# A second pair of PSUM banks for the attention output, and the weight sums moved from head pair 2 to head pair 7

## The reference, cut to what matters

```python
qkv = grouped_linear(x, w_qkv, None)              # 8 groups, 128 -> 384
attn = softmax((q * D**-0.5) @ k^T)               # 16 heads, D = 64
x = layernorm(x + grouped_linear(attn @ v, w_proj, b_proj))
def _weight_quant(w):
    scale = 1.0 / clip(mean(abs(w)), 1e-05)
    return clip(round(w * scale), -1.0, 1.0) / scale
def _bitlinear(x, w): return einsum('bsi,oi->bso', _act_quant(x), _weight_quant(w))
x = layernorm(x + _bitlinear(silu(_bitlinear(x, w_gate)) * _bitlinear(x, w_up), w_down))
```

## Time and profile before

| | us |
|---|---|
| median of 2 runs | 2174.44 |
| the profiled execution, device time | 2174.42 |
| its span on the slowest core (core 2), first to last instruction | 2171.6 |
| PE busy / ACT busy / DVE busy | 1345.0 / 969.3 / 924.0 |
| attention and its projections, from about 190 to 1183 us of the span | about 990 |
| FFN, from about 1196 us on | about 975 |

### The profile page before, as it was taken

One profiled execution on the slowest core, in us unless ns is written; L12 is line 12 of the kernel. 1 busy time (PEld: TensorE's weight loads), 2 busy tenths in 40 slices (PEclk: granted clock), 3 DMA queues, 4 the chain that ended last, 5 costly groups with the idle time before them and its releaser, 6 DMA issues.

```text
span 2171.6 us, 20607 instructions; the slowest of 8 cores (2159.1 to 2171.6 us)
## 1 busy us (share of the span) xinstructions
PE 1345.0 (62%) x5502; PEld 462.6 (21%) x5502; DVE 924.0 (43%) x1742; ACT 969.3 (45%) x1079; POOL 44.6 (2%) x84
## 2 busy tenths in 40 slices
PE   0057666466656665045663599964999847676682
PEld 0011111111111111011111244421444312222231
DVE  1138840463548344385515644444444441203023
ACT  2167778477866877037782122255121352011011
POOL 0000000000000000001000000000000000000000
PEclk9999888688877888568886799987999978898896
DMA  6789950124752587745721533334244425676672
GB/s 190 215 237 311 321 178 1 34 79 128 200 143 78 168 225 218 212 122 169 216 61 37 143 78 78 76 99 136 51 95 97 107 97 155 162 208 182 183 210 82
DMA packets 371458, 314.02 MB, mean 145 GB/s; under 512 B 296593, under 2 KB 298641, under 8 KB 369298
## 3 DMA queue, kind: packets, MB, share of 16 engines
q1 hardware_dynamic: 339712, 234.97, 41.8%
q10 hardware_dynamic: 23186, 48.38, 6.3%
q0 software_dynamic: 8448, 29.37, 3.5%
HBM read 161.49 MB, written 83.89 MB: 113 GB/s over the span
## 4 chain that ended last, share of the span: by engine, by line
PE 36%; ACT 21%; DMA 13%; DVE 12%; SPq 8%; issue 7%; ACTq 2%; DVEq 1%; POOL 0%; POOLq 0%
PE ps L84 36%; ACT A L84 21%; DVE A L84 8%; SPq L84 7%; DMA A<-wg 3%; DMA wdt_sb<-wdqT_s 2%; DVE ln_sb L84 2%; ACTq L84 2%; DMA wtstage<-wdq_s 2%; DMA A<-wproj 1%; DMA xre_f<-xp_s 1%; DVE h L84 1%; DMA wdqT_s<-wtstage 1%; DMA A<-wu 1%; DMA A<-x 1%
## 5 line engine op out<-in xcount | busy, mean ns | idle before, releaser
L84 ACT ACTIVATE A<-ps,cst_sb 128x1024 bf16<-128x1024 f32 (+1 forms) x544 | 573.7, 1087 | 276.4 <-DVE A L84 143.6
L84 PE MATMUL ps<-A,A 128*65 128x512 bf16 (+1 forms) x2048 | 527.8, 427 | 271.9 <-ACT A L84 258.5
L84 PE MATMUL ps<-wg_sl,xqT 128*128 128x512 bf16 x1024 | 266.4, 407 | 114.4 <-DVE h L84 101.1
L84 PE MATMUL ps<-wdt_sb,hqT 128*128 128x512 bf16 x1024 | 242.4, 396 | 106.6 <-DMA wdt_sb<-wdqT_s 50.2
L84 PEld LDWEIGHTS ps<-A,A 128*65 128x65 bf16 (+1 forms) x2048 | 124.8, 105 | 673.1 <-issue 673.1
L84 ACT ACTIVATE A<-ps,scg 128x512 f32<-128x512 f32 x128 | 87.9, 687 | 332.2 <-PE ps L84 310.2
L84 DVE SCALAR_TENSOR_TENSOR h<-ps,scu,A 128x512 bf16<-128x512 f32 x128 | 96.1, 750 | 217.3 <-ACT A L84 213.1
L84 DVE TENSOR_SCALAR A<-A,wsc 128x1024 f32<-128x1024 f32 x96 | 72.2, 753 | 212.4 <-DMA A<-wg 100.9
L84 DVE TENSOR_SCALAR A<-A 128x1024 f32<-128x1024 f32 (+1 forms) x208 | 144.3, 694 | 32.1 <-DVE A L84 18.0
L84 PEld LDWEIGHTS ps<-wg_sl,xqT 128*128 128x128 bf16 x1024 | 103.9, 103 | 252.8 <-issue 146.3
L84 PEld LDWEIGHTS ps<-wdt_sb,hqT 128*128 128x128 bf16 x1024 | 100.8, 101 | 248.2 <-issue 145.8
(11 more groups left out here) (66 smaller groups left out, 702.2 us busy)
## 6 DMA issues: line engine op xcount, KB each, us to landing
A<-wg SPq DMA_DIRECT2D x64, 512.0 KB, 6.5
A<-wu SPq DMA_DIRECT2D x64, 512.0 KB, 5.7
A<-wd SPq DMA_DIRECT2D x64, 512.0 KB, 6.7
wdt_sb<-wdqT_s SPq DMA_DIRECT2D x128, 256.0 KB, 3.2
hq_s<-h ACTq DMA_DIRECT2D x16, 1024.0 KB, 3.9
A<-x SPq DMA_DIRECT2D x16, 512.0 KB, 7.7
xt_s<-A POOLq DMA_DIRECT2D x16, 512.0 KB, 4.2
A<-xt_s ACTq DMA_DIRECT2D x16, 512.0 KB, 3.3
```

The lines of the kernel that those rows point to most:

```text
L84: ins = getattr(eng, meth)(*args, **kw)
```

## The change

Three things are edited. The PV matmuls and the four copies use PSUM banks 4 and 5 for even head pairs and banks 6 and 7 for odd ones, and the first PV matmul of a pair waits only until the copies of the pair before the last are done (`c_pve` less 1). The weight sums (`emit_wsum`) are taken after pair 7 of query chunk 1 and no longer after pair 2; since `drain_wq` runs only once they are taken, and only for p < 7, the units begin at pair 0 of query chunk 2. And since the sums use PSUM bank 6, waits are added: the sums wait for all copies, the first PV matmul and the projection for `wsc`.

```diff
     def emit_wsum():
         wait("tensor", "c_bpb", 1)
+        wait("tensor", "c_pve", c("c_pve"))
         wait("tensor", "c_wma", c("c_wma"))
...
         for p in range(8):
+            pvb = 2048 if p % 2 == 0 else 3072
...
                 if kc == 0:
-                    wait("tensor", "c_pve", c("c_pve"))
-                if kc == 0 and p == 0:
+                    wait("tensor", "c_pve", max(0, c("c_pve") - 1))
+                    wait("tensor", "c_wsc", c("c_wsc"))
+                if kc == 0 and p <= 1:
                     wait("tensor", "c_radd", c("c_radd"))
                 va = A4[:, kc * 1040:(kc + 1) * 1040]
-                em("tensor", "matmul", ps[0:65, 2048:2560],
+                em("tensor", "matmul", ps[0:65, pvb:pvb + 512],
...
-            em("scalar", "copy", arp[0:64, :], ps[0:64, 2048:2560])
-            em("scalar", "copy", arp[64:128, :], ps[0:64, 2560:3072])
+            em("scalar", "copy", arp[0:64, :], ps[0:64, pvb:pvb + 512])
+            em("scalar", "copy", arp[64:128, :], ps[0:64, pvb + 512:pvb + 1024])
...
-            if qc == wsum_qc and p == 2:
+            if qc == wsum_qc and p == 7:
                 emit_wsum_once()
...
             xre = A0[:, par * 1024:(par + 1) * 1024]
             wait("tensor", "c_rcp", c("c_rcp"))
+            wait("tensor", "c_wsc", c("c_wsc"))
```

More of the change, by code:

```diff
@@ L682, in build @@
                    start=(kc == 0), stop=(kc == T - 1))
-                em("tensor", "matmul", ps[0:65, 2560:3072],
+                em("tensor", "matmul", ps[0:65, pvb + 512:pvb + 1024],
                    va[:, 65 * (2 * p + 1): 65 * (2 * p + 1) + 65],
@@ L700, in build @@
             arp = A8[:, p * 512:(p + 1) * 512]
-            em("scalar", "copy", arp[0:64, :], ps[0:64, 2048:2560])
-            em("scalar", "copy", arp[64:128, :], ps[0:64, 2560:3072])
+            em("scalar", "copy", arp[0:64, :], ps[0:64, pvb:pvb + 512])
+            em("scalar", "copy", arp[64:128, :], ps[0:64, pvb + 512:pvb + 1024])
             em("scalar", "copy",
                A9[row:row + 1, 0:512].rearrange("r (q tc) -> r tc q", tc=4),
-               ps[64:65, 2048:2560])
+               ps[64:65, pvb:pvb + 512])
             em("scalar", "copy",
                A9[row:row + 1, 512:1024].rearrange("r (q tc) -> r tc q", tc=4),
-               ps[64:65, 2560:3072], inc=("c_pve", 1))
+               ps[64:65, pvb + 512:pvb + 1024], inc=("c_pve", 1))
             if attn_lvl < 2:
```

## The result

| | before | after |
|---|---|---|
| median, us | 2175.22 (8 runs) | 2260.37 (9 runs) |
| ratio, 95% interval | 1 | 1.0389 [1.0369, 1.0409] |
| span of the slowest core in the profiled execution | 2171.6 (core 2) | 2265.3 (core 0) |

The change makes the kernel 3.9 per cent slower. 2270 us were forecast, in a range of 2250 to 2290.

A forecast was written before the change was run, and what follows sets the result against it. ACT paces the attention, but chunk 2's end waits for weight quantization units and transposes. Sums -2.0, chunk 2 -30.3, chunk 3 +58.8 and tail +69.0 give +95.5 on 2174.4: 2270 us, range 2250 to 2290.

The forecast's parts named there:

- The banks: 0: Pair changes in attention: new banks gain 0, since ACT's copies stand ahead of the exp that the first PV matmul needs.
- The bound of -39 us: Lower bound for the banks: some 1.4 us of ACT idle time taken away at each of 28 pair changes.
- The bound of +3 us: Upper bound for the banks: one more semaphore to look at per pair, at most a tenth of a us.
- The weight sums: -2.0: Chunk 1: 2.4 us go at pair 2, 0.4 come back at pair 7, so it ends 2.0 us earlier.
- Chunk 2: reciprocal at 897.3: End of chunk 2: w_down's 32 units come first, reciprocal at 897.3 in place of 929.57; -30.3 us in the sum.
- Chunk 3: +58.8: Chunk 3 takes the load chunk 2 had, 208.05 us; reciprocal at 1185.5 in place of 1159.05.
- The tail: +69.0: Behind the last layer norm: 12 units and the weight load it hid, less 17 us of waiting.
- the landing of the last store: In the tail: the last unit's store lands in 4.7 us, and only then may SP transpose the first weight slices.
- a restart at the lower clock: FFN slice 0: eight matmuls took 3.57 us where 1.89 is usual; this goes, 1.7 us less.
- A: Pair changes: the banks do help, PE takes up work and ACT follows; 39 us less, 2231 us; chance 0.03.
- B: Reciprocal of chunk 3: units hide behind the attention if under 3.5 us each with transposes; 58.7 us less, 2211 us; chance 0.05.
- C: Tail worse: units at 4.0 us, slice 2 late, slow store; +5, +3, +5, 2283 us; within the forecast's 0.87.

The follow-up runs named there:

- experiment 1: Changed kernel with the weight sums back at pair 2 of chunk 1, leaving only the second banks and relaxed wait: 2179.47 us, ratio 1.0001.
- experiment 5: Kernel before with the second banks, and a pair's copies and DMA issues put behind the next pair's second exp (pair 7 excepted): 2172.98 us, ratio 0.9972.
- experiment 9: Kernel before with sums after pair 7 of chunk 0, units spread 38, 29, 29 and w_down transposes in the FFN: 2130.21 us, ratio 0.9776.
- 10: Kernel before with second banks, deferred copies, balanced units, w_down transposes in the FFN, next pair's first two score matmuls behind PV 14 and 15: 2095.93 us, ratio 0.9615.
- Experiment 2: Kernel before, old banks, with the weight sums and all units moved to pair 7 of chunk 1: 2264.56 us, ratio 1.0382.
- Experiment 4: Changed kernel with the 32 w_down transposes moved from the attention to the FFN, 2 behind each slice load: 2211.05 us, ratio 1.0131.
- Experiment 3: Changed kernel with 8 units per pair in chunk 3 instead of 6, none left behind the last layer norm: 2241.92 us, ratio 1.0276.
- 6: Kernel before, old banks, with sums after pair 7 of chunk 0 and units spread 38, 29, 29, transposes 8, 14, 10: 2128.65 us, ratio 0.9772.

## Why the prediction was right

**The banks: 0.** Right, by experiment 1. The reason given (the copies stand on ACT ahead of the exp that the PV matmul needs) is confirmed from both sides: PE's wait is unchanged, and with another order on ACT (experiment 5) the first PV matmuls do pass the copies. But the reason was half of it: even then banks and order together gave 6 us, since the copies take ACT's own time. The bound of -39 us counted idle time of ACT that the banks do not reach; it took PE's order too to get to some 34 us (experiments 9 and 10: 2130.21 - 2095.93). The bound of +3 us rested on a tenth of a us for one more semaphore wait, which no run shows by itself; with that wait in it, experiment 1 is at 1.0001.

**The weight sums: -2.0.** The stage took 1.2 us less on the slowest core, and over the eight cores it fell from a mean of 232.0 to 229.8 us. At the end of chunk 1 PE now waits for the sums:

```profile
643.14 0.40 PE L84 MATMUL ps<-wproj_sb,A 64*128 64x128 bf16 x4 [0.46 <-ACT wsc L84]
```

Before, it waited for the reciprocal:

```profile
640.61 0.40 PE L84 MATMUL ps<-wproj_sb,A 64*128 64x128 bf16 x4 [6.75 <-DVE A L84]
```

The 0.46 us are not the price. The projection starts 0.80 us behind the reciprocal (643.14 - 642.34) where it was 0.70 (640.61 - 639.91), so the chain costs 0.1 us there and not the 0.4 taken.

**Chunk 2: reciprocal at 897.3.** It came at 897.96, from a start 4.4 us later than assumed (the reciprocal of chunk 1 at 642.34 for 637.9), so the stage was 3.7 us shorter than forecast. Of this, 2.9 us lie ahead of the first unit, which came 84.5 us behind the reciprocal of chunk 1 (87.4 forecast). The w_down units took 4.0 us each as in chunk 1. Experiment 2 gives the same waits without the banks.

**Chunk 3: +58.8.** 55.7 measured. The argument that it would be the chunk 2 of before was the best step of the prediction, since it needed no price. It is not "exactly the load of chunk 2 before", though: the number of units and of blocks is the same, but they are 22 w_gate and 20 w_up tiles, where chunk 2 before had 2 of w_down, 32 of w_gate and 8 of w_up. From the end of the tokens' transposes to the reciprocal it took 204.7 us where 208.05 were carried over. Two w_down units at 4.0 us for 3.46 are 1.1 us of that; the rest is open. Experiment 4 shows the cause in it, the transposes on SP. That the earlier trace rows show each block with DVE idle was read into them: of the two rows of transposes there one is a block, and the idle time is in the row of 917.03 at experiment 4.

**The tail: +69.0.** 66.1 measured, the row of 1286.14 standing 36.9 us behind 1249.21 (37.7 forecast). The term mis-sized is the landing of the last store, 4.7 us taken and 2.0 measured. The trace of before had the right number: of its 32 stores of w_up the last two, issued at 1096.3 and 1099.7, landed in 2.0 us each (the view of tile wuq_s in that window).

A second, smaller miss goes the other way. The prediction took 1.7 us off for a restart at the lower clock. Before, from the first up matmuls on, PE comes out of a wait twice at a granted clock of 0.50 (1.2 GHz): at 1206.59, where eight matmuls take 3.1 us for 1.7 at a granted clock of 1.00, and at 1228.82, where sixteen take 5.7 us for 3.5. After, it does so once, at 1313.11, but there sixteen matmuls take 6.3 us (1313.11 to 1319.44). So 0.8 us went and not 1.7, and slice 0 took 28.8 us from there and not 28.0. Experiment 3 confirms that hiding the weight load behind the layer norm was worth about 21 us.

**Rivals.** A fell by experiment 1. B described the right place and the right condition (a unit with its share of transposes under 3.5 us), and experiment 4 shows it come true once the transposes are gone. C didn't come: units and store were at or under their price, and from slice 1 to the end the mean over the eight cores is 0.7 us less than before.

The median of 2260.37 lies 9.5 us under the forecast. In the means over the eight cores the three large stages were over-priced by 2.7, 5.1 and 3.7 us, 11.5 in all. These three errors lie on one side, and the range of 2250 to 2290 was wide enough to hold their sum.

## What to carry to other kernels

When background work is moved within a list that engines follow in order, its cost isn't the work but the deadline that it now stands ahead of: count the units ahead of each point where another engine waits, and compare with the room there. A new stretch that has nearly the same list as a known one can be priced by the rows of the known one; check what in it differs. Before pricing a second buffer, look which instruction releases the waiting one. If it stands behind the copies on the engine that empties the first buffer, the second is worth nothing as it is, and if that engine sets the pace, little even with another order. And a median is a poor price for the last transfer of a row: look at the last ones by themselves.

## What the runs showed that was not expected

The transposes of w_down hold up the units beside them where these stand ahead of a deadline that is late: 24 of them made the end of chunk 3 some 55 us later, and all 32 cost 8.5 us in the FFN (mean over the eight cores), 2 behind each slice load (experiment 4). With the units balanced the same move gains nothing in all: what it takes off chunk 1 it adds to the FFN (experiment 9 beside 6).

And a landing time depends on what stands beside the transfer: in both traces the last two stores of w_up, the only ones that SP issues with no load of a tile beside them, landed in 2.0 us, where the median of the 32 in the trace of before is 4.7. Whether it is the load that makes the difference was not tested.
